# Causal mask of an attention kernel's maximum pass: added by the vector engine in PSUM instead of by mask products on TensorE

## The reference, cut to what matters

```python
scores = jnp.einsum('bqhrd,bkhd->bhrqk', q, k) * scale
causal = jnp.tril(jnp.ones((Tq, Tq), dtype=bool))
scores = jnp.where(causal, scores, jnp.finfo(scores.dtype).min)
probs = jax.nn.softmax(scores, axis=-1)
y = jnp.einsum('bhrqk,bkhd->bqhrd', probs, v)
x = x + y.reshape(Bq, Tq, N_HEADS * HEAD_DIM) @ wo
```

## Time and profile before

| what | us |
|---|---|
| median of 3 runs | 460.65 (460.63 to 463.32) |
| the profiled execution, whole | 460.89 |
| its span | 459.2 |
| PE busy | 413.5 (90%) |
| DVE busy | 280.7 (61%) |
| ACT busy | 250.5 (55%) |
| POOL busy | 225.1 (49%) |

### The profile page before, as it was taken

How to read it: one execution, slowest core, us unless ns; L and a number is a source line. 1 busy time by engine, 2 the same in 40 slices (tenths; PEclk the granted TensorE clock), 3 DMA queues, 4 the chain that set the end, 5 groups by cost and what they waited for, 6 DMA issues and landing times.

```text
span 459.2 us, 6945 instructions
## 1 busy us (share of the span) xinstructions
PE 413.5 (90%) x2556; PEld 244.2 (53%) x2556; DVE 280.7 (61%) x426; ACT 250.5 (55%) x484; POOL 225.1 (49%) x186
## 2 busy tenths in 40 slices
PE   5888889999999999999999999999999998989991
PEld 3573556555655565545655565545656474533541
DVE  6256865656657466556967476553966486614546
ACT  2423337655566665655665665555745656567640
POOL 2002132366635862376635852376336945586352
PEclk9967989999999999999999999999999999999997
DMA  6684900375014601065034601065052601001011
GB/s 207 150 104 124 140 3 1 120 184 79 1 33 55 89 1 47 14 86 77 1 84 52 87 2 47 13 97 66 1 99 35 87 2 47 1 2 47 0 48 46
DMA packets 20609, 27.35 MB, mean 60 GB/s; under 512 B 2528, under 2 KB 12768, under 8 KB 20448
## 3 DMA queue, kind: packets, MB, share of 16 engines
q1 hardware_dynamic: 19712, 25.43, 30.7%
q10 hardware_dynamic: 864, 1.48, 0.9%
HBM read 6.72 MB, written 4.19 MB: 24 GB/s over the span
## 4 chain that ended last, share of the span: by engine, by line
PE 66%; DVE 11%; POOL 7%; ACT 6%; issue 6%; DMA 2%; SPq 0%; DVEq 0%; POOLq 0%; ACTq 0%
PE u_ps L565 13%; PE st_ps L519 12%; PE mx_ps L540 11%; PE sh_ps L576 7%; PE sh_ps L626 6%; PE sh_ps L670 5%; DVE mx_part L966 5%; POOL pr L1288 5%; ACT pr L800 3%; PE mx_ps L546 3%; PE sh_ps L619 2%; DMA qs<-q_lo 2%; POOL pr L1275 1%; PE sh_ps L655 1%; PE sh_ps L611 1%
## 5 line engine op out<-in xcount | busy, mean ns | idle before, releaser
L966 DVE TENSOR_REDUCE mx_part<-mx_ps 128x2 f32<-128x1024 f32 (+3 forms) x160 | 175.4, 1114 | 93.9 <-PE mx_ps L546 55.7
L800 ACT ACTIVATE pr<-st_ps 128x512 f32<-128x512 f32 (+1 forms) x304 | 166.9, 574 | 88.3 <-PE st_ps L519 78.2
L1288 POOL TENSOR_TENSOR pr<-pr 128x768 f32<-128x768 f32 (+4 forms) x60 | 144.4, 2410 | 66.5 <-PE u_ps L565 43.8
L519 PE MATMUL st_ps<-qs,ks 98*128 98x512 f32 (+1 forms) x304 | 140.1, 470 | 10.5 <-ACT pr L800 10.0
L540 PE MATMUL mx_ps<-ks,qs 96*128 96x512 f32 (+3 forms) x384 | 110.6, 369 | 5.3 <-DVE mx_part L966 3.7
L1275 POOL TENSOR_SCALAR_AFFINE_SELECT pr<-pr 128x512 f32<-128x512 f32 x64 | 40.8, 638 | 115.1 <-ACT pr L800 114.9
L519 PEld LDWEIGHTS st_ps<-qs,ks 98*128 98x128 f32 x304 | 56.9, 188 | 63.3 <-ACT pr L800 36.2
L540 PEld LDWEIGHTS mx_ps<-ks,qs 96*128 96x128 f32 x384 | 70.2, 195 | 23.6 <-DVE mx_part L966 9.6
L565 PE MATMUL u_ps<-pr,v 128*32 128x512 f32 (+3 forms) x768 | 72.3, 492 | 1.5 <-POOL pr L1275 1.5
L546 PE MATMUL mx_ps<-mask_r,ident_r 128*128 128x128 f32 (+2 forms) x176 | 46.2, 262 | 0.0
L565 PEld LDWEIGHTS u_ps<-pr,v 128*32 128x32 f32 x768 | 20.1, 109 | 36.9 <-issue 28.6
(11 more groups left out here) (109 smaller groups left out, 329.9 us busy)
## 6 DMA issues: line engine op xcount, KB each, us to landing
qs<-q_hi SPq DMA_DIRECT2D x32, 256.0 KB, 5.6
qs<-q_lo SPq DMA_DIRECT2D x16, 256.0 KB, 6.7
out_y<-y SPq DMA_DIRECT2D x7, 512.0 KB, 3.1
x<-in_x SPq DMA_DIRECT2D x3, 1024.0 KB, 7.9
ks<-k_hi SPq DMA_DIRECT2D x32, 64.0 KB, 5.3
x<-in_x SPq DMA_DIRECT2D x4, 256.0 KB, 5.6
pr<-in_wq ACTq DMA_DIRECT2D x1, 1024.0 KB, 7.6
ks<-k_lo SPq DMA_DIRECT2D x16, 64.0 KB, 5.9
```

The costliest lines, as they stand in the source:

```text
L519: nc.tensor.matmul(st_ps[n % 2][:, 0:nh * width], ks[g][0:KM, kt * P:(kt + 1) * P], qs[g][0:KM, c, h0:h0 + nh, off:CH], start=True, stop=T ...
L800: nc.scalar.activation(pr[:, slot, h0:h0 + nh, off:CH], st_ps[n % 2][:, 0:nh * width].rearrange("p (h q) -> p h q", h=nh), ACT.Exp, scale= ...
L966: nc.vector.tensor_reduce(mx_part[:, t // CT, own, h0:h0 + nh, t % CT], mx_ps[n % 2][:, 0:nh * pitch].rearrange("p (h k) -> p h k", h=nh)[ ...
L1288: last = nc.gpsimd.tensor_tensor(even, even, pr[:, 6 + (e // 2) % 2, h0:h1, off:CH], ALU.add)
```

## The change

Each head's score product now stands by itself (`start=True, stop=True`), PE's mask products are left out, and DVE adds the mask (`mask_r`, 128 columns for each head) to the diagonal blocks in the PSUM buffer itself before it reduces. The add signals a new semaphore `masked`, on which DVE waits ahead of the reduce. Everything else, the order of the units and the tables included, is as it was. `mask_r` and `ident_r` remain; PE's warm-up products (L690) still use them.

```diff
+OWN_UNITS = [n for n, u in enumerate(MX) if u[3]]
+NOWN = len(OWN_UNITS)
...
+        masked = sem("masked")
...
-                together = max(1, CH // pitch) if own else 1
-                for i0 in range(0, nh, together):
-                    heads = range(i0, i0 + together)
-                    for i in heads:
-                        last = nc.tensor.matmul(bank[:, i * pitch:i * pitch + width],
-                                                qs[g][0:KS, t // CT, h0 + i, t % CT * P:(t % CT + 1) * P],
-                                                ks[g][0:KS, k0:k0 + width], start=i == i0, stop=not own)
-                    if own:
-                        diagonals = bank[:, i0 * pitch:(i0 + together) * pitch].rearrange(
-                            "p (h k) -> p h k", h=together)[:, :, width - P:width]
-                        last = nc.tensor.matmul(diagonals, ident_r[:, :], mask_r[:, 0:together, :], start=False, stop=True)
+                for i in range(nh):
+                    last = nc.tensor.matmul(bank[:, i * pitch:i * pitch + width],
+                                            qs[g][0:KS, t // CT, h0 + i, t % CT * P:(t % CT + 1) * P],
+                                            ks[g][0:KS, k0:k0 + width], start=True, stop=True)
                 last.then_inc(mx_full, 1)
...
-                nc.vector.tensor_reduce(mx_part[:, t // CT, own, h0:h0 + nh, t % CT],
-                                        mx_ps[n % 2][:, 0:nh * pitch].rearrange("p (h k) -> p h k", h=nh)[:, :, 0:width],
-                                        AX.X, ALU.max).then_inc(mx_free, 1)
+                scores = mx_ps[n % 2][:, 0:nh * pitch].rearrange("p (h k) -> p h k", h=nh)[:, :, 0:width]
+                if own:
+                    diagonals = scores[:, :, width - P:width]
+                    nc.vector.tensor_tensor(diagonals, diagonals, mask_r[:, 0:nh, :].bitcast(F), ALU.add
+                                            ).then_inc(masked, 1)
+                    dve.wait_ge(masked, w * NOWN + OWN_UNITS.index(n) + 1)
+                nc.vector.tensor_reduce(mx_part[:, t // CT, own, h0:h0 + nh, t % CT], scores, AX.X, ALU.max
+                                        ).then_inc(mx_free, 1)
```

## The result

The change made the kernel slower: 481.7 us against 460.6 us in the median, ratio 1.044 (95% interval 1.038 to 1.049). The forecast was 467.6 us in a range of 461 to 477. The direction was right, the forecast loss was a third of what came. The profiled execution took 483.3 us with a span of 481.5.

A forecast was written before the change was run, and what follows sets the result against it. PE is busiest (90%), but DVE's queue at the readings PE's next fills need was taken to decide. 1.2 + 2.3 - 0.5 + 3 x 0.4 + 2 x 1.4 = +7.0 us gave 467.6 us, range 461 to 477.

The forecast's parts named there:

- PE's saving: Maximum pass without mask products: PE saves 2.2 us a window, 18 us over eight windows.
- DVE's delay at sum1: Adds make mx_lo, which sum1 needs, later: +0.45 us where g = 0, +0.9 us where g = 1.
- The start: Six own units ahead of m0: adds bring 3.2 us, pauses and an earlier-full first unit take up part; +1.2 us.
- Window 0's passage: Six own units among DVE's reduces in window 0 bring 3.2 us, about 1 us taken up: +2.2 us.
- Window 1: DVE has room without scale_half and add_half; m1 comes later, the other units save: -0.5 us.
- the g = 0 and g = 1 steps: Windows 2, 4, 6 (g = 0) net +0.4 us each; windows 3, 5 (g = 1) net +1.4 us each.
- Rival C: PE's clock drops to 1.2 GHz in start and sparse stretch, 1.7 us each; two more give 471 us; chance 0.12.
- the forecast's own list of new gaps: Expected signs: sum1 waits for mx_lo in every window; m0 for reciprocals (g = 1, 1 to 2 us) or f3's reading (g = 0).
- The waits at m0: DVE's adds delay the readings m0 waits for: +0.9 us where g = 0, +1.9 us where g = 1.
- A: PE's saving wins, six windows keep 2.2 us each if adds are cheap: 451 us; chance 0.08.
- B: Dearer adds, 0.12 us more per own unit at start, window 0, sum1 and m0: +5.8 us, 473 us; chance 0.17.
- D: Waits for ACT absorb the later windows' lateness; only start and window 0 cost: 464 us; chance 0.25.

The follow-up runs named there:

- x6: The changed kernel without any mask in the maximum pass and with DVE reading m1 ahead of unit t = 1: median 457.5 us, ratio 0.985.
- x4: The changed kernel with DVE reading the fill m1 ahead of unit t = 1 instead of behind it: median 468.5 us, ratio 1.017.
- x10: The changed kernel with masks of four-head units back on PE, DVE adding only for two-head units: median 464.4 us, ratio 1.003.
- x3: The changed kernel with six unneeded PE products ahead of the wait for sum1 in windows 1 to 6: median 477.4 us, ratio 1.034.
- x8: The kernel before with two unneeded DVE reduces ahead of reading m1 in windows 0 to 6: executions of 470.5, 473.8, 480.5 and 971 us, no ratio.
- x11: The changed kernel with the masks of windows 0 and 1 on PE, adds from window 2 on: median 476.7 us, ratio 1.029.
- x5: The kernel before with DVE reading the fill m1 ahead of unit t = 1: median 462.1 us, ratio 1.000.
- x1: The changed kernel without the adds, so no mask at all in the maximum pass: median 454.3 us, ratio 0.985.

## Why the prediction was wrong, by its own steps

**Right.** Adds of 688 and 426 ns, and the reduce 0.03 to 0.04 us behind, all 96 times (267.64 + 0.70 = 268.34, then 268.38). PE's saving: without mask products and at a like clock PE is busy 396.9 us in x6, 16.6 us less than before; I had 18. DVE's delay at sum1: from mark to sum1 4.34 instead of 3.37 us in window 3, 5.09 instead of 4.57 in window 4, so 0.97 and 0.52 us, forecast 0.9 and 0.45. The start from its first product to m0: 28.08 to 38.15 us against 26.39 to 35.66, +0.8 us, forecast 1.2. Window 0's passage without the clock: +2.3 us, forecast 2.2. Window 1: from second to third mark 48.4 instead of 49.2 us, -0.8, forecast -0.5.

**The step that failed** is the one that let PE's own durations stand while its waits grew: the g = 0 and g = 1 steps priced the gap ahead of sum1 by its length alone. That gap, which the forecast had put in its place and size, came with PE at 1.2 GHz on sum1 in each of windows 2 to 6, and where the gap was taken away (x4, x10) or filled (x3), sum1 there ran at full clock. The five sum1 of windows 2 to 6 took 4.91, 4.67, 4.91, 6.03 and 6.11 us instead of 3.21 each, 10.6 us in all, against 7.0 forecast for the whole change. The rest of those windows was forecast well: 13.9 us less 10.6 leaves 3.3, and the forecast had 3 x 0.4 + 2 x 1.4 = 4.0. Window 0 lost another 3.0 us to the clock by my estimate and window 7 1.7, but kernels that have no adds there lost the clock at these places too (x8 and x11 in window 0, x5 in window 7), so they aren't counted here. Rival C named this mechanism and priced one stretch well (1.7 us), but looked for it in the start and window 0 alone and gave it two stretches and a chance of 0.12. Its condition should have taken in every new gap next to the products that PE loses, and the forecast's own list of new gaps had one per window.

**Mis-sized.** The waits at m0. I had +1.0 us there for g = 1 beyond sum1 (1.9 less 0.9) and +0.45 for g = 0. From sum1 to m0 window 3 takes 20.05 us (220.53 to 240.58) instead of 18.63, which is 1.42 us more, and sum1's slow clock explains 1.46 of it; in window 4 it is 20.93 instead of 19.19, 1.74, of which sum1 1.70. So in these two windows the adds ahead of m0 cost nothing beyond what PE saves. In windows 5 and 6 they do: m0 comes 3.51 and 3.98 us later behind sum1 than before, of which sum1 is 2.82 and 2.90, so 0.7 and 1.1 us are left. x4, with sum1 at full clock, has the same, 18.43 instead of 17.73 us and 19.23 instead of 18.17. So the forecast was too high in windows 3 and 4, near in window 5 and too low in window 6. The reciprocals are waited for (0.52 us in window 3, 1.12 in window 5). In window 3 DVE had got time back: L1046 (L1045 before) took 1.36 us, where it took 2.53 before, and 1626 ns in the mean instead of 2038. That it overlaps less with POOL's work is a guess that no run tests.

**Chance.** 1.7 us of the profiled execution (its first maximum product at 28.08 instead of 26.39 us) come ahead of any changed instruction, from a low stretch at 15.2 us. x5 has one at 16 us too and is as fast as the kernel before, so I don't count it to the change.

The rivals: A fell; x1 shows what its saving is worth without the adds (1.5%), and x4 that with the adds and m1 read first only 1.7 us are left of it in windows 2 to 6. B fell, the adds cost the forecast's price. D fell, the lateness at sum1 was not absorbed. The Trainium skill's rule that a semaphore between chained operations of VectorE costs nothing (VectorE: DVE Perf Modes, "The DRAIN you can't avoid") isn't borne out here either: the reduce starts 0.04 us behind the add's end, while operations without a wait start 0.1 us ahead of it.

**What stays open.** When the clock falls is not settled. The gap and the missing mask products each make it likelier in these traces, but they don't decide it: window 1 of the changed kernel had both and kept its clock. Window 7 has no maximum units in any kernel and PE waits 0.51 and about 1.35 us for ACT ahead of its sum1 in every one; three of the thirteen profiled executions kept the clock there and ten lost it. Nor are the 6 us spread of x1 and x6, the clock's part in window 0 and that of window 7 explained.

## What to carry to other kernels

When a change puts a new wait in front of a busy TensorE, price it twice: its length, and half of the time that the engine may then run at 1.2 GHz (here 1.7 us for a stretch of 3.4 us), for every place where the wait recurs. Moving work off the busiest engine can lose if the receiving engine's queue has a reading behind the new work that the first one needs at once; look for that reading first, since moving it ahead of the new work (two lines here) recovered 13 of 21 us. And ask whether the work is needed at all: without any mask in the maximum pass the kernel is 1.5% faster than before (interval 0.7% to 2.2%).

## What the runs showed of the hardware that was not expected

Behind a gap of only 0.56 us ahead of sum1 PE's clock fell for 3.4 us (window 4 after), when PE had waited 0.80 and 0.58 us for ACT within the 6 us before it and had no mask products; a gap of 1.49 us was borne twice in x8. The same program can do either from one execution to the next: x1 ran at 451 and at 457 us with a clock of 0.967 and 0.952. Feeding PE six unneeded products per window made the kernel 4 us faster. An addition of VectorE that reads and writes PSUM costs the same 688 ns for 512 columns as one that writes SBUF (689 ns).
